# Placements of the attention parts issued from ScalarE's program in each batch's front

## The reference, cut to what matters

```python
qg = hidden_states @ Wq
q, gate = (qg[..., :H * D], qg[..., H * D:])
k = hidden_states @ Wk
q = _apply_partial_rope(q, cos, sin)
k = _apply_partial_rope(k, cos, sin)
scores = jnp.einsum('bkgsd,bktd->bkgst', qg4, k) / jnp.sqrt(jnp.asarray(D, q.dtype))
attn = jax.nn.softmax(scores, axis=-1)
out = jnp.einsum('bkgst,bktd->bkgsd', attn, v)
```

## Time and profile before

| What | Value |
|---|---|
| Time, median of 3 runs | 1774.87 us (1772.9 to 1777.85) |
| Time of the profiled execution | 1773.95 us |
| Its span, first to last instruction | 1772.1 us |
| TensorE busy | 1674.5 us (94%) |
| VectorE busy | 1378.8 us (78%) |
| POOL busy | 1030.5 us (58%) |
| ScalarE busy | 710.5 us (40%) |
| Mean granted clock of TensorE | 0.976 |

### The profile page before, as it was taken

The page is one execution under the profiler, slowest core; times in us unless marked ns, Lnnn a source line. Parts: engine busy times, 40 slices in busy tenths (PEclk is TensorE's granted clock), DMA queues, the critical chain, the costliest instruction groups (busy, mean ns, idle before and its releaser), DMA issues.

```text
span 1772.1 us, 24588 instructions
## 1 busy us (share of the span) xinstructions
PE 1674.5 (94%) x6902; PEld 858.6 (48%) x6902; DVE 1378.8 (78%) x1692; ACT 710.5 (40%) x895; POOL 1030.5 (58%) x765
## 2 busy tenths in 40 slices
PE   5699999999999999999878999999999999999996
PEld 3444444444444444447744444444444444444685
DVE  6678888878887787757767778888888888886587
ACT  1234444444444443444332444444444444444352
POOL 0556666666666665654344666666666666657342
PEclk9789999999999999999887999999999999999998
DMA  4600001111111100020043000010000000000001
GB/s 163 160 14 23 23 23 25 24 26 27 27 24 24 25 20 1 1 77 25 25 115 82 23 23 23 23 24 23 22 22 23 22 22 22 19 1 1 24 25 48
DMA packets 36906, 59.68 MB, mean 34 GB/s; under 512 B 6624, under 2 KB 17264, under 8 KB 36288
## 3 DMA queue, kind: packets, MB, share of 16 engines
q1 hardware_dynamic: 36800, 58.50, 12.6%
HBM read 20.07 MB, written 4.19 MB: 14 GB/s over the span
## 4 chain that ended last, share of the span: by engine, by line
PE 75%; DVE 12%; issue 7%; POOL 3%; DMA 2%; ACT 1%; SPq 0%; DVEq 0%; POOLq 0%; ACTq 0%
PE ob L568 23%; PE sc L553 14%; PE sc L556 11%; PE mx L526 11%; PE misc L506 6%; PE mx L665 3%; DVE acc L323 2%; DVE maxp L1040 2%; POOL acc L323 2%; PE misc L579 1%; DVE maxp L1178 1%; PE sc L632 1%; PE ob L680 1%; DMA acc<-in_x 1%; DVE oge L1069 1%
## 5 line engine op out<-in xcount | busy, mean ns | idle before, releaser
L323 POOL TENSOR_TENSOR acc<-acc,probs 128x512 f32<-128x512 f32 x448 | 602.8, 1346 | 365.8 <-DVE acc L323 353.4
L1040 DVE TENSOR_REDUCE maxp<-mx 128x2 f32<-128x1024 f32 x468 | 567.1, 1212 | 232.3 <-PE mx L528 225.8
L820 ACT ACTIVATE probs<-sc 128x1024 f32<-128x1024 f32 x512 | 501.2, 1025 | 574.5 <-PE sc L556 574.5
L568 PE MATMUL ob<-probs,v_sb 128*64 128x512 f32 x2048 | 496.3, 605 | 0.5 <-ACT probs L820 0.5
L323 DVE TENSOR_TENSOR acc<-acc,probs 128x512 f32<-128x512 f32 x448 | 422.8, 944 | 23.5 <-ACT probs L820 22.6
L553 PE MATMUL sc<-qa,kab 128*128 128x512 f32 x1024 | 351.1, 424 | 0.0
L556 PE MATMUL sc<-qb,kab 128*128 128x512 f32 x1024 | 320.8, 394 | 0.0
L526 PE MATMUL mx<-kab,qa 64*128 64x512 f32 x490 | 248.4, 507 | 32.3 <-DMA kab<-high_sb 12.4
L528 PE MATMUL mx<-kab,qa 64*128 64x512 f32 x490 | 247.9, 506 | 0.0
L526 PEld LDWEIGHTS mx<-kab,qa 64*128 64x128 f32 x490 | 91.1, 186 | 295.3 <-issue 153.1
L568 PEld LDWEIGHTS ob<-probs,v_sb 128*64 128x64 f32 x2048 | 124.0, 136 | 212.6 <-issue 149.7
(11 more groups left out here) (130 smaller groups left out, 1549.0 us busy)
## 6 DMA issues: line engine op xcount, KB each, us to landing
qa<-high_sb SPq DMA_DIRECT2D x128, 128.0 KB, 2.3
qb<-low_sb SPq DMA_DIRECT2D x64, 128.0 KB, 2.3
tables_sb<-in_tables SPq DMA_DIRECT2D x34, 128.0 KB, 2.4
xT_sb<-in_xT SPq DMA_DIRECT2D x2, 2048.0 KB, 9.4
acc<-in_x SPq DMA_DIRECT2D x8, 512.0 KB, 4.1
out_y<-acc SPq DMA_DIRECT2D x8, 512.0 KB, 3.2
kab<-acc SPq DMA_DIRECT2D x24, 128.0 KB, 2.4
rot_sb<-raw_sb SPq DMA_DIRECT2D x72, 32.0 KB, 1.8
```

Of the source, the lines that this page charges most:

```text
L323: ops.tensor_tensor(total, total, part, ALU.add).then_inc(summed, 1)
L568: mm = nc.tensor.matmul(ob[hd * D:(hd + 1) * D, :], v_sb[:, t, kv * D:(kv + 1) * D], probs[:, k % RING, hd * CHUNK:(hd + 1) * CHUNK], star ...
L820: nc.scalar.activation(probs[:, k % RING, :].rearrange("p (h n) -> p h n", h=2), sc[:, 2 * (k % 2):2 * (k % 2) + 2, :], ACT.Exp, scale=flo ...
L1040: nc.vector.tensor_reduce(two_columns(p, j), mx[:, :, :], AX_X, ALU.max).then_inc(maxed, 1)
```

## The change

The placements of the seven front stages leave SyncE's program and enter ScalarE's. The function `place` takes the engine as an argument and, with the functions that name the targets, moves ahead of the engines' programs. Each place stands in ScalarE's order where the list below has it; it has the same wait, the same six DMAs and the same semaphores as before. The waits, the DMAs and the buffers of all other steps stay as they are, and the placements inside the attention steps stay on SyncE.

```diff
+        def place(eng, stage, b, targets):
+            slot = stage[0]
+            eng.wait_ge(low_done[slot], done(uses(stage, b) + 1))
+            for part, hd, dst in targets:
+                src = raw_words(part[slot][hd * D:(hd + 1) * D])
+                eng.dma_start(raw_words(dst), src).then_inc(placed[slot], 16)
...
+        def front_targets(s):
+            what, n = FRONT[s][0:2]
+            return k_targets(n) if what == "k" else q_targets(n)
...
-                        place(behind(p, c), b, q_targets((p + AHEAD) % PAIRS))
+                        place(sp, behind(p, c), b, q_targets((p + AHEAD) % PAIRS))
...
                 front_swap(2)
                 front_tables(3)
                 front_swap(3)
-                front_place(0)
-                front_place(1)
                 front_tables(4)
                 front_swap(4)
                 front_tables(5)
-                front_place(2)
                 front_swap(5)
-                front_place(3)
-                front_place(4)
                 front_tables(6)
                 front_swap(6)
-                front_place(5)
-                front_place(6)
                 place_max(b, 0, 0)
...
+                def front_place(s):
+                    place(act, front(s), b, front_targets(s))
+
                 for s in range(SLOTS):
                     front_copy(s)
                 front_round(0)
                 front_copy(4)
+                front_place(0)
                 front_round(1)
                 copy_v(0, b)
                 copy_v(1, b)
                 front_copy(5)
+                front_place(1)
                 front_round(2)
+                front_place(2)
                 front_round(3)
+                front_place(3)
                 front_round(4)
+                front_place(4)
                 copy_v(2, b)
                 front_copy(6)
                 copy_v(3, b)
                 front_round(5)
+                front_place(5)
                 front_round(6)
+                front_place(6)
                 attention_steps(act, step(b))
```

More of the change, by code:

```diff
@@ L323, in add_exponentials, with k_targets, q_targets @@
                 ops.tensor_tensor(total, total, part, ALU.add).then_inc(summed, 1)
+        def place(eng, stage, b, targets):
[4 more added lines that the diff above has]
+                eng.dma_start(raw_words(dst), src).then_inc(placed[slot], 16)
+        def k_targets(n):
+            keys = slice(n * CHUNK, (n + 1) * CHUNK)
+            return [t for g in range(KVH) for t in (
+                (high, g, ka[0:D, g, keys]), (low, g, ka[D:P, g, keys]), (high, g, kb[D:P, g, keys]))]
+        def q_targets(slot):
+            return [t for hd in range(2) for t in (
+                (high, hd, qa[0:D, slot, hd, :]), (high, hd, qa[D:P, slot, hd, :]), (low, hd, qb[D:P, slot, hd, :]))]
+        def front_targets(s):
+            what, n = FRONT[s][0:2]
+            return k_targets(n) if what == "k" else q_targets(n)
         FRONT_BANKS = [misc, ob]
@@ L363, in swap_rows @@
                     sp.dma_start(rot[slot][to::8], raw[slot][frm::8]).then_inc(rot_placed[slot], 16)
[L365 to L382, removed]
             def place_max(b, c, p):
@@ L417, in front_swap @@
                     swap_rows(front(s), s, b)
-                def front_place(s):
-                    what, n = FRONT[s][0:2]
-                    place(front(s), b, k_targets(n) if what == "k" else q_targets(n))
                 front_swap(0)
```

## The result

| | before | changed |
|---|---|---|
| Median | 1775.01 us (1771.13 to 1778.03, 20 runs) | 1777.97 us (1772.79 to 1781.85, 20 runs) |
| Ratio, 95% interval | | 1.0017 [1.0009, 1.0025] |
| Profiled execution, its span | 1773.95, 1772.1 us | 1777.7, 1775.7 us |

The changed kernel is 0.17% slower, 1.6 to 4.4 us by the interval and 2.96 us by the medians. That lies inside the 0.3% that was called no change, and beside the forecast of +2.75.

What follows compares the result with a forecast made beforehand. TensorE bounds attention; in the two fronts it waits, with place 1's placements on the path. Batch 0's +2.0 us and batch 1's +0.75 make +2.75, on the median 1774.87 giving 1777.6 us; range 1773.5 to 1784.5.

Steps and rivals of the forecast that it cites:

- Removed from SyncE: SyncE's queue: taking away 42 placement DMAs per batch by itself gains nothing.
- The price of an issue: ScalarE's queue: a placement DMA costs SyncE's price there, median 596 ns.
- Rival 2: ScalarE's queue: issues cheaper, 0.46 us each, sum -1.4 us, 1773.5; chance 0.06.
- Term A: Front, ScalarE: round 1 stands behind place 0's issues, +1.47 us in batch 0 and +0.2 in batch 1.
- Term B: Front, ScalarE: place 1 stands behind two V copies and copy 5, about +0.05 us per batch, 0.6 at worst.
- Term C: Front, DMA engines: SyncE's freed table and swaps, 192 KB, meet place 1; +0.5 us per batch, bounds 0 and 0.95.
- Late next: Front, places behind place 1: not the bound, place 2 has 1.6 us slack; place 5 adds 0.3 at worst.
- Sum: Both fronts: batch 0 +2.0 us, batch 1 +0.75, together +2.75 us.
- Rival 1: Fronts: issues of SyncE's and ScalarE's queues hold each other up, sum 8.2 us, 1783.1; chance 0.28.
- Rival 3: Fronts: place 0 takes 3.7 us, SyncE's traffic fills gaps; +1.0 us, 1775.9; chance 0.62 together with the forecast.

Runs made afterwards that it cites:

- E2: Changed kernel with places 0 and 1 back on SyncE, places 2 to 6 staying on ScalarE; ratio to the kernel before 1.0002.
- E3: Kernel before with only place 0 moved to ScalarE, places 1 to 6 staying on SyncE; ratio 1.0032.
- E7: Repeat of E3, only place 0 on ScalarE against the kernel before; ratio 1.0024.
- E1: Changed kernel, but SyncE holds stage 4's table and all later tables and swaps until place 1 has landed; ratio to the kernel before 1.0010.
- E5: Kernel before, with the two key DMAs the row maxima need issued first and waited for alone; ratio 0.9983.
- E4: Changed kernel with place 0 back on SyncE, places 1 to 6 on ScalarE; ratio to the kernel before 1.0021.
- E9: Changed kernel with the two key DMAs the row maxima need issued first and waited for alone; ratio to the kernel before 1.0012.
- E10: Repeat of E5, the kernel before with the needed key DMAs first; ratio 0.9975.
- E6: Kernel before with place 1 split, three DMAs each from SyncE and ScalarE, and stage 4's table held until place 1 landed; ratio 1.0013.
- E8: The changed kernel run again unaltered, against the kernel before; ratio 1.0015.

## Why the prediction came out as it did

**Removed from SyncE: nothing.** Right: E2, with five of seven places moved, is as fast as before within 0.12%.

**The price of an issue.** Right: 0.618 to 0.624 us median on ScalarE, 0.596 on SyncE. Rival 2 needed 0.46.

**Term A**, forecast 1.47 and 0.2. The mechanism is right: in the changed kernel the issues released round 1 in both batches, and E3 and E7 show it alone in batch 0. (E1 doesn't, as VectorE's rope ended as late there.) The size was low: the two profiles give 2.20 and 1.45 in batch 0, 0.81 and 0.50 in batch 1. The step that failed is "with that length on ScalarE": SyncE's 4.28 and 4.06 were taken over, and place 0 took 4.23 to 4.97. They were to stand for stage 4's table and swaps as well, but in the kernel before these come only from 58.26 on the earlier trace rows, behind place 0. What they add isn't settled. Without them place 0 took 3.75 to 3.91 on ScalarE (E1), but on SyncE with no issue of ScalarE's beside it anything from 3.69 (E5) to 5.27 (E4).

**Term B**, forecast 0.05. Right: from round 1 to place 1's first issue it was 1.68 and 1.67 us and is 1.96 and 1.46, then 1.65 and 1.52. The row at 49.14 shows a DMA issued while a copy runs.

**Term C**, forecast 0.5 between bounds 0 and 0.95. The place and the cause are right, the choice of the middle was not: 0.87, 0.92, 0.92 and 0.75 us. With the traffic gone it is 0.06 or less (E1, E3, E7), with twice the traffic 0.99 to 1.45 (E4). The 192 KB of the other queue cost the product nearly all of their 0.95 us; the "gaps" that might have taken half of them are not there. The Trainium skill, page "DMA: Bandwidth & Descriptors", section on queues, rings and completion order, says that SyncE and ScalarE each own a ring on each of the same 16 DMA engines and no engines of their own. The trace agrees: 192 KB on one queue delay the other's by 0.75 to 0.92, near 192 KB / 208 GB/s = 0.95.

**Late next.** That places 2, 3, 4 and 6 have slack was right, and so was "0.3 at worst" for place 5 (0.44 became 0.54). But "round 5 follows copy 6 there as before" left out that copy 6 itself now follows place 4. While place 1 is late, that second cost is covered, but for the 0.1 us of place 5. In E1 and E9 it shows: TensorE waits 1.73 to 2.89 us for place 5, where it waited for nothing in batch 0 and 0.44 us in batch 1 before.

**Sum.** The marks grew by 3.35 + 1.52 = 4.87 us, in the second profile by 2.34 + 1.10 = 3.44, for 2.75 forecast; the times grew by 3.0 [1.6, 4.4] and 2.7 [1.2, 4.3]. The forecast met the time better than it met its own terms, and that is luck. What takes 1 or 2 us back isn't settled. It is not the rest of the fronts: from the first product to the first exponential batch 0 is longer than before (34.49 and 35.49, for 33.66) and batch 1 shorter (33.69 and 33.81, for 34.49), so that copy 4 to first exponential grew by 4.90 and 4.59 us in all. The profiles have 1.94 and 1.53 us less between batch 0's first exponential and batch 1's copy 4, but there E5 and E10, one kernel, differ by 5.2 us. And E3 and E7 cost more time than their marks, so the times are not the sum of the marks in any case.

**Rival 1** (queues take turns, +8.2) is refuted as to its price. Its sign is there: place 1's six issues take 3.94 to 4.04 us beside three of SyncE's, 3.71 without (E1). That is 0.2 to 0.3 us, not three slots of 0.62; and in E6 three issues on each queue ran side by side. The sign that the prediction named for it, DMAs stretched above 0.6 us, did show in place 0 (1.73 us at 50.36). But in the kernel before two issues took 1.71 us and in E4 2.70 (50.09), with SyncE issuing alone, so that stretch needs no second queue. The Trainium skill, page "Perfetto Trace Analysis", section on the HWDGE DMA instruction, says that one sequencer locks the generator of descriptors for itself while it uses it, and that the profiled issue holds the wait for it. The trace leaves room for a short lock only: with six issues done in 2.03 us it can be held for 0.34 us of an issue at most, an estimate from E6. **Rival 3** needed the traffic to be hidden, and it isn't.

## What to carry to other kernels

Where a wait on the path is for a landing, count the bytes that any queue puts in flight at that moment (192 KB cost nearly their whole transfer time here); moving the issue to another engine frees its old queue to send earlier, and that traffic is the price. An issue written into a computing engine's program takes 0.62 us of that engine's order, so look at every instruction behind it, also those that today wait for something else. When a landing sets the end, let the consumer wait for the parts that it reads, and issue these first: that gave 0.17 and 0.25% here, and the change of queue cost 0.17 and 0.15%.

## What the runs showed of the hardware

**VectorE beside POOL.** The last rope step on VectorE in batch 0 took 0.69 us in one profile of the changed kernel and 1.64 in the other. VectorE's timeline of E8, then POOL's:

```profile
49.84 0.68 DVE L294 TENSOR_TENSOR rot_sb<-rot_sb,tables_sb 128x512 f32<-128x512 f32 x1
50.56 1.64 DVE L299 TENSOR_TENSOR raw_sb<-raw_sb,rot_sb 128x512 f32<-128x512 f32 x1
```

```profile
49.97 1.68 POOL L293 TENSOR_TENSOR probs<-probs 128x512 f32<-128x512 f32 x1 [44.78 <-DMA probs<-probs]
51.62 1.71 POOL L294 TENSOR_TENSOR probs<-probs 128x512 f32<-128x512 f32 x1
```

In the first profile POOL began only at 53.03 and VectorE's step at 50.34 was not stretched. With both at work each slows (POOL 1.26 alone). The Trainium skill, page "GPSIMD Engine Reference", section on specifications, says that POOL shares its SBUF interfaces with VectorE and contends with its instructions of two SBUF inputs; the trace agrees. So a swap that lands earlier on POOL's side can lengthen the path on VectorE's, by about 1 us a step: the longer rope shows in E2's batch 1, E4's batch 0 and both batches of E1. In E2's batch 1 POOL began 0.71 us ahead of copy 4, in the kernel before 0.43 behind it.

**The clock after a pause.** TensorE's third projection of batch 1 in E7, and in E10:

```profile
907.91 3.78 PE L509 MATMUL misc<-xT_sb,wk_sb 128*128 128x512 f32 x4 [4.30 <-ACT raw_sb L791]
```

```profile
899.04 2.79 PE L517 MATMUL misc<-xT_sb,wqg_sb 128*128 128x512 f32 x4 [3.47 <-issue]
...
905.22 1.98 PE L517 MATMUL misc<-xT_sb,wk_sb 128*128 128x512 f32 x4 [0.81 <-ACT raw_sb L801]
```

After a pause of 4.30 us the four matmuls took 3.78 us, at half clock (granted 0.50, 1.2 GHz), after 0.81 they took 1.98, at full. E10 is not free of the fall, it has it earlier: its first projection, at 899.04 behind 3.47 us of idle time, took 2.79 us (granted 0.51 from 900 to 902 us), and the pause behind it was the shorter for it. In E5, the same kernel as E10, the pause was 4.45 us and from copy 0 to copy 4 it took 9.56 us instead of 6.80. A like fall stands behind attention in E3 and not in the kernel before (windows, clock third from the end):

```profile
795.00:800.00 5.00, 4.43 (x12) 3.21 (x12) 1.29 (x2) 1.67 (x3) 0.83 (x1) 0.66 0.01 2
```

```profile
795.00:800.00 5.00, 5.00 (x24) 4.05 (x23) 1.66 (x3) 2.86 (x6) 2.81 (x3) 1.00 0.01 2
```

Such stretches, 2 to 3 us each, are as large as the effect that was to be measured; that is why the terms were read from marks in the front and not from the spans.
